# First quad of the feed-forward pass prepared in the last steps of the image pass, its global net beside layer 1 (vision tower, one core)

## The reference, cut to what matters

```
h = h + attention(layernorm(h))        # 16 heads of 16, low-rank projections, causal softmax
x = layernorm(h)                       # feed-forward pass starts here
gf = sigmoid(gelu(gelu(mean_t(x) @ gc_w1 + gc_b1) @ gc_w2 + gc_b2) @ gc_w3 + gc_b3)   # global net
out = x
for _ in range(3):                     # cycles
    tf = sigmoid(mlp4(out))            # 256 -> 256 -> 128 -> 64 -> 1, gelu between
    coupling = 0.1 + adaptive_range * (0.7 * gf + 0.3 * tf - 0.5) * 2
    out = out + coupling * twist(out)  # twist permutes and negates quarters of the row
h = h + out
```

## Time and profile before

| what | value |
|---|---|
| median of 3 runs | 3767.67 us |
| the profiled execution's own time | 3769.01 us |
| its span | 3767.3 us |
| granted TensorE clock, mean | 0.99 of full speed |
| PE busy | 3644.8 us, 97% |
| DVE busy | 3028.1 us, 80% |
| ACT busy | 2402.5 us, 64% |
| POOL busy | 1830.5 us, 49% |
| share of PE in the chain that ended last | 81% |

### The profile page before, as it was taken

One profiled execution on the slowest core, in us unless ns is written; L12 is line 12 of the kernel. 1 busy time (PEld: TensorE's weight loads), 2 busy tenths in 40 slices (PEclk: granted clock), 3 DMA queues, 4 the chain that ended last, 5 costly groups with the idle time before them and its releaser, 6 DMA issues.

```text
span 3767.3 us, 83941 instructions
## 1 busy us (share of the span) xinstructions
PE 3644.8 (97%) x29710; PEld 2685.5 (71%) x29710; DVE 3028.1 (80%) x7295; ACT 2402.5 (64%) x5698; POOL 1830.5 (49%) x2960
## 2 busy tenths in 40 slices
PE   6999999999999999999999999996999999999998
PEld 5888888888888887888888888874555555555554
DVE  6777777777777777777777777774898998998996
ACT  3777777777777777777777777773455555454454
POOL 3766676666667666666766667664100100100000
PEclk9999999999999999999999999997999999999999
DMA  3444454444444444444444444443221222222211
GB/s 103 132 120 125 125 132 119 124 127 126 122 121 132 120 122 128 127 122 121 132 127 122 124 128 131 120 105 95 64 74 58 80 69 63 79 66 68 79 44 52
DMA packets 200000, 398.18 MB, mean 106 GB/s; under 512 B 28192, under 2 KB 133920, under 8 KB 199584
## 3 DMA queue, kind: packets, MB, share of 16 engines
q1 hardware_dynamic: 199584, 392.81, 38.4%
HBM read 131.80 MB, written 53.26 MB: 49 GB/s over the span
## 4 chain that ended last, share of the span: by engine, by line
PE 81%; DVE 9%; issue 3%; POOL 3%; ACT 2%; DMA 2%; SPq 0%; DVEq 0%; POOLq 0%; ACTq 0%
PE ps L1048 14%; PE ps L1326 11%; PE ps L1135 8%; PE ps L1083 7%; PE ps L1335 6%; PE ps L1096 6%; PE ps L1162 4%; PE ps L1120 4%; PE ps L1169 4%; PE ps L1143 3%; PE ps L1164 3%; PE ps L1350 2%; PE ps L1342 2%; POOL p L473 2%; PE ps L1058 1%
## 5 line engine op out<-in xcount | busy, mean ns | idle before, releaser
L1048 PE MATMUL ps<-xb,w_tok 128*128 128x196 f32 x3072 | 694.8, 350 | 0.8 <-DVE h L773 0.5
L857 DVE TENSOR_REDUCE mx<-ps 128x4 f32<-128x512 f32 x512 | 352.5, 688 | 364.6 <-PE ps L1164 364.6
L1326 PE MATMUL ps<-X,cn_w 128*128 128x394 f32 x1536 | 584.9, 510 | 0.4 <-issue 0.4
L861 DVE TENSOR_REDUCE mx<-ps 69x2 f32<-69x396 f32 x1024 | 528.8, 556 | 0.0
L557 ACT ACTIVATE p<-ps 128x394 f32<-128x394 f32 x1024 | 454.6, 499 | 76.4 <-PE ps L1096 66.8
L1048 PEld LDWEIGHTS ps<-xb,w_tok 128*128 128x128 f32 x3072 | 487.1, 190 | 1.2 <-DVE h L773 0.8
L537 POOL TENSOR_SCALAR ve<-mv 128x4 f32<-128x4 f32 x64 | 19.8, 310 | 920.4 <-DVE mv L917 920.4
L1326 PEld LDWEIGHTS ps<-X,cn_w 128*128 128x128 f32 x1536 | 274.1, 190 | 250.7 <-issue 95.4
L508 POOL TENSOR_TENSOR h<-h,att 128x256 f32<-128x256 f32 (+1 forms) x256 | 186.8, 749 | 533.5 <-DVE att L850 533.5
L1169 PE MATMUL ps<-kZ,qT 128*69 128x396 f32 x1024 | 397.2, 454 | 0.1
L1096 PE MATMUL ps<-qZ,kT 128*128 128x396 f32 (+1 forms) x2048 | 380.4, 319 | 11.3 <-DMA qZ<-mx_scratch 8.4
(11 more groups left out here) (140 smaller groups left out, 8238.4 us busy)
## 6 DMA issues: line engine op xcount, KB each, us to landing
kZ<-kT SPq DMA_DIRECT2D x512, 198.0 KB, 3.6
qZ<-qT SPq DMA_DIRECT2D x256, 396.0 KB, 4.7
xb<-in_x SPq DMA_DIRECT2D x128, 588.0 KB, 6.6
h_scratch<-h SPq DMA_DIRECT2D x128, 128.0 KB
hl<-h_scratch SPq DMA_DIRECT2D x64, 256.0 KB
hk<-h_scratch SPq DMA_DIRECT2D x64, 256.0 KB
out<-hk SPq DMA_DIRECT2D x64, 256.0 KB
h_scratch<-h SPq DMA_DIRECT2D x128, 69.0 KB
```

Of the source, the lines that this page charges most:

```text
L857: v.tensor_reduce(mx[:, 0, 4 * i:4 * i + 4], ps[:, b0, :].rearrange("p (a b) -> p a b", b=P), AX.X, ALU.max, negate=True).then_inc(s_max, 1)
L861: v.tensor_reduce(mx[:T1, 1, 4 * i + 2 * jj:4 * i + 2 * jj + 2], ps[:T1, b, 0:2 * TE].rearrange("p (a b) -> p a b", b=TE), AX.X, ALU.max, ...
L1048: mm = t_.matmul(ps[:, W[ft], 0:NP], w_tok[:, k, ft * P:ft * P + P], xb[:, par, k, :], start=k == 0, stop=k == KT - 1)
L1326: mm = t_.matmul(ps[:, 2 * c + mt, 0:N2], cn_w1[:, f, mt * P:mt * P + P], X[:, c, state(cyc), f, :], start=f == 0, stop=f == FT - 1)
```

## The change

SP issues the `hl` loads of quad 0 at the end of step B-2, when the h1 stores of images 0 to 7 are known to have landed; they go to SBUF space of their own, as do `hn2`, `st2`, `ve2`, `rstd2`. DVE does `stats2(0, 0..3)` and `apply2(0, 0..1)` in step B+1 behind `attend`, and `apply2(0, 2..3)` in step B+2 behind the last `attend`. POOL does `norm2(0, 0..1)` in step B+1 in front of the four `select` and `norm2(0, 2..3)` behind them. PE waits for the last `att_ready` before its first `x_transpose`, since the PSUM banks are shared. The three layers of the first global net move into the first phase, between layer-1 and layer-2 matmuls, on PSUM banks given by `GB0`; the wait for g_ready moves to the second phase. The `hk` loads stay behind the wait for all h1 stores.

```diff
--- before.py
+++ after.py
@@ -154,13 +154,7 @@
-        hl = sb("hl", [P, 4, 2, 2, D])
-        st2 = sb("st2", [P, 4, 4, 6])
-        ve2 = sb("ve2", [P, 4, 4])
-        rstd2 = sb("rstd2", [P, 4, 4])
-        hn2 = sb("hn2", [P, 4, 4, D])
-
@@ -174,6 +168,12 @@
+
+        hl = sb("hl", [P, 4, 2, 2, D])
+        hn2 = sb("hn2", [P, 4, 4, D])
+        st2 = sb("st2", [P, 4, 4, 6])
+        ve2 = sb("ve2", [P, 4, 4])
+        rstd2 = sb("rstd2", [P, 4, 4])
@@ -266,6 +266,8 @@
 
         QUADS = B // 8
 
+        GB0 = ((5, 6), (7, 4), (5, 6))
+
         def phases():
 
             for i in range(QUADS):
@@ -360,6 +362,11 @@
...
+            def load2(dst, i, c, s):
+                for t in range(2):
+                    src = h1_dram[:, t * P:t * P + TS[t], :].rearrange("(g n) p d -> g p n d", n=2)
+                    sp.dma_start(dst[0:TS[t], c, t, :, :], src[i * 4 + c]).then_inc(s[c], 16)
+
@@ -378,19 +385,17 @@
                 if there(n + 5):
                     sp.wait_ge(tok_done, n * 2 + 8)
                     load_x(n + 5, 1 - r % 2)
+                if n == B - 2:
+                    for p2 in range(2):
+                        sp.wait_ge(h1_stored[p2], 16 * 8 + 1)
+                    for c in range(4):
+                        load2(hl, 0, c, hl_loaded)
 
             images(sp, step)
             for par in range(2):
                 sp.wait_ge(h1_stored[par], 16 * B + 1)
 
 
-            def load2(dst, i, c, s):
-                for t in range(2):
-                    src = h1_dram[:, t * P:t * P + TS[t], :].rearrange("(g n) p d -> g p n d", n=2)
-                    sp.dma_start(dst[0:TS[t], c, t, :, :], src[i * 4 + c]).then_inc(s[c], 16)
-
-            for c in range(4):
-                load2(hl, 0, c, hl_loaded)
             for c in range(4):
                 load2(hk, 0, c, hk_loaded)
 
@@ -508,15 +513,28 @@
                     g.tensor_tensor(h1[:M, r % 2, t, :], h[:M, m % 6, t, :], att[:M, t, :], ALU.add)\
                      .then_inc(h1_ready, 1)
 
+            def norm2(i, c):
+
+                wait(mv2_ready[c // 2], i * 8 + 4 * (c % 2) + 4)
+                g.tensor_scalar(ve2[:, c, :], mv2[:, c, :, 1], LN_EPS, None, ALU.add).then_inc(ve2_done[c // 2], 1)
+                pool.wait_ge(ve2_done[c // 2], i * 2 + c % 2 + 1)
+                g.tensor_tensor(rstd2[:, c, :], ve2[:, c, :], power[:, 0:4], ALU.pow).then_inc(rstd2_done[c // 2], 1)
+
             def step(n, r):
                 if there(n - 3):
                     residual(n - 3, (r + 1) % 4)
+                if n == B + 1:
+                    norm2(0, 0)
+                    norm2(0, 1)
                 if there(n):
                     k_weighted(n, r, 0)
                     k_weighted(n, r, 1)
                 if there(n - 2):
                     for i in range(4):
                         select(n - 2, i)
+                if n == B + 1:
+                    norm2(0, 2)
+                    norm2(0, 3)
                 if there(n):
                     k_low_part(n, r, 0)
                     q_low_part(n, r, 0)
@@ -531,14 +549,7 @@
...
-            def norm2(i, c):
...
-            for i in range(QUADS):
+            for i in range(1, QUADS):
                for c in range(4):
                     norm2(i, c)
@@ -656,16 +667,17 @@
                     copy(X[:, c, 0, f, :], ps[:, 2 * c + f, 0:N2]).then_inc(x_ready[c], 1)
 
             def gnet(i, G, l):
-                b = 4 * G
+                b1 = GB0[l][G] if i == 0 else 4 * G + 1
+                b2 = GB0[l][G] if i == 0 else 4 * G + 2
                 act.wait_ge(g_done[G], i * 3 + l + 1)
                 if l == 0:
-                    s.activation(ga1[:, G, :], ps[:G1, b + 1, 0:4], ACT.Gelu, bias=gc_b1[:, 0:1],
+                    s.activation(ga1[:, G, :], ps[:G1, b1, 0:4], ACT.Gelu, bias=gc_b1[:, 0:1],
                                  scale=1.0 / T).then_inc(g_ready[G], 1)
                 elif l == 1:
-                    s.activation(ga2[:, G, :], ps[:G2, b + 2, 0:4], ACT.Gelu, bias=gc_b2[:, 0:1])\
+                    s.activation(ga2[:, G, :], ps[:G2, b2, 0:4], ACT.Gelu, bias=gc_b2[:, 0:1])\
                      .then_inc(g_ready[G], 1)
                 else:
-                    s.activation(gth[:, G, :], ps[:, b + 2, 0:4], ACT.Tanh, bias=gc_b3[:, 1:2], scale=0.5)\
+                    s.activation(gth[:, G, :], ps[:, b2, 0:4], ACT.Tanh, bias=gc_b3[:, 1:2], scale=0.5)\
                      .then_inc(g_ready[G], 1)
 
             def gelu1(i, cyc, c):
@@ -690,28 +702,33 @@
 
             for c in range(4):
                 x_copy(0, c)
-            for l in range(3):
-                for G in range(2):
-                    gnet(0, G, l)
+            def gnet0(start, l):
+                if start:
+                    for G in range(2):
+                        gnet(0, G, l)
 
             for i, cyc, G, oi, ocyc in phases():
                 O = 1 - G
+                start = oi < 0
                 fresh = ocyc == CYCLES - 1 and oi + 1 < QUADS
                 if oi >= 0:
                     gelu3(oi, ocyc, O)
                     if fresh:
                         gnet(oi + 1, O, 1)
                 gelu1(i, cyc, 2 * G)
+                gnet0(start, 0)
                 if oi >= 0:
                     for c in (2 * O, 2 * O + 1):
                         tanh(oi, ocyc, c)
                     if fresh:
                         gnet(oi + 1, O, 2)
                 gelu1(i, cyc, 2 * G + 1)
+                gnet0(start, 1)
                 if oi >= 0 and ocyc == 1 and oi + 1 < QUADS:
                     for c in (2 * O, 2 * O + 1):
                         x_copy(oi + 1, c)
                 gelu2(i, cyc, 2 * G)
+                gnet0(start, 2)
                 if cyc == CYCLES - 1 and i + 1 < QUADS:
                     gnet(i + 1, G, 0)
                 gelu2(i, cyc, 2 * G + 1)
@@ -862,6 +879,26 @@
...
+            def stats2(i, c):
...
+            def apply2(i, c, first):
...
@@ -871,6 +908,14 @@
                     rms_sum(n, 1)
                 if there(n - 3):
                     attend(n - 3)
+                if n == B + 1:
+                    for c in range(4):
+                        stats2(0, c)
+                    apply2(0, 0, True)
+                    apply2(0, 1, True)
+                if n == B + 2:
+                    apply2(0, 2, True)
+                    apply2(0, 3, True)
                 if there(n):
                     rms_small(n)
                 if there(n + 2):
@@ -906,26 +951,6 @@
...
-            def stats2(i, c):
...
-            def apply2(i, c, first):
...
@@ -981,10 +1006,6 @@
                     v.tensor_tensor(y, y, ps[:M, 2 * c + t, :].rearrange("p (n d) -> p n d", n=2), ALU.add)\
                      .then_inc(y_ready[c], 1)
 
-            for c in range(4):
-                stats2(0, c)
-            for c in range(4):
-                apply2(0, c, True)
             for c in range(4):
                 gsums(0, c)
             for G in range(2):
@@ -1301,16 +1322,17 @@
                     mm.then_inc(x_done[c], 1)
 
             def gnet(i, G, l):
-                b = 4 * G
+                b1 = GB0[l][G] if i == 0 else 4 * G + 1
+                b2 = GB0[l][G] if i == 0 else 4 * G + 2
                 if l == 0:
                     pe.wait_ge(gsum_ready[G], i * 2 + 2)
                     for f in range(FT):
-                        mm = t_.matmul(ps[:G1, b + 1, 0:4], gc_w1[:, f, :], gsum[:, G, f, :], start=f == 0,
+                        mm = t_.matmul(ps[:G1, b1, 0:4], gc_w1[:, f, :], gsum[:, G, f, :], start=f == 0,
                                        stop=f == FT - 1)
                 else:
                     pe.wait_ge(g_ready[G], i * 3 + l)
-                    mm = t_.matmul(ps[:G2, b + 2, 0:4], gc_w2[:], ga1[:, G, :], start=True, stop=True) if l == 1 else \
-                        t_.matmul(ps[:, b + 2, 0:4], gc_w3r[:], ga2[:, G, :], start=True, stop=True)
+                    mm = t_.matmul(ps[:G2, b2, 0:4], gc_w2[:], ga1[:, G, :], start=True, stop=True) if l == 1 else \
+                        t_.matmul(ps[:, b2, 0:4], gc_w3r[:], ga2[:, G, :], start=True, stop=True)
                 mm.then_inc(g_done[G], 1)
 
             def layer1(i, cyc, c, f):
@@ -1362,18 +1384,23 @@
                                               X[:, c, state(CYCLES), f, n * T + t * P:n * T + t * P + M], ident[:, :])
                     mm.then_inc(y_done[c], 1)
 
+            pe.wait_ge(att_ready, 2 * B)
             for c in range(4):
                 x_transpose(0, c)
-            for c in range(4):
-                pe.wait_ge(x_ready[c], 2)
-            for l in range(3):
-                for G in range(2):
-                    gnet(0, G, l)
-            for G in range(2):
-                pe.wait_ge(g_ready[G], 3)
+
+            def gnet0(start, l):
+                if start:
+                    for c in (2, 3):
+                        pe.wait_ge(x_ready[c], 2)
+                    for G in range(2):
```

(8 more changed lines are left out.)

36 lines of the change are left out of this document (16 added, 20 removed).

## The result

The changed kernel takes 3755.53 us (median of 5 runs, 3755.38 to 3758.79), the kernel before in the same comparison 3770.06 us (5 runs, 3766.25 to 3778.0). The ratio is 0.9966, 95% interval 0.9955 to 0.9978: faster, by 0.34%. The forecast was 3756.6 us, range 3750 to 3762, which is 11.1 us less than before; the medians are 14.5 us apart.

The account below looks back on a forecast made before the run. PE, busy 97%, was taken as the bound, with one large hole at the seam. 18.2 - 1.8 - 4.0 - 1.0 - 0.3 = 11.1 us off 3769.0 gave 3757.9, by the median 3756.6 us; range 3750 to 3762.

Parts of the forecast that it names:

- Term 1: Seam between image pass and feed-forward: layer 1 of cycle 1 earlier, limited by quad 1's hl loads; 18.2 us gained.
- Rival B: At the seam: quad 1's loads flow faster and don't hold DVE; 15.8 us gained, 3751.9 us; chance 0.05.
- Term 2: Layer 1 of cycle 1: PE at low clock behind the new gap in front of it; 1.8 us lost.
- Rival D: Feed-forward pass: the new gap leaves PE at half clock for whole phases; slower, 3777.2 us; chance 0.04.
- Term 3: Step B-2: the mx_scratch store waits behind eight hl loads on SP's queue, delaying scoresT; 4.0 us lost.
- Rival A: Step B-2: small transfers pass the loads, so the store doesn't wait; 16.1 us gained, 3751.6 us; chance 0.11.
- Term 4: Scores and pv behind scoresT: low clock after the longer gap in front of scoresT; 1.0 us lost.
- Term 5: Step B+1: POOL's two norm2 in front of select make PE's selects late; 0.3 us lost.

Follow-up runs that it names:

- the repeat of after: The changed kernel run again without edits, beside three further kernels on the same chip: 3751.88 us against 3766.59 for the kernel before, ratio 0.9963.
- the repeat of before: The kernel before the change, run once more without edits for its profile: 3767.96 us (one run).
- the norms late: The changed kernel with quad 0's statistics, norm2 and apply2 back behind the last attend, loads still early: 3757.34 us against 3769.06, ratio 0.997.
- the global net alone: The changed kernel with quad 0's loads, statistics and norms back behind the image pass, global net still beside layer 1: 3767.84 us, ratio 0.9988.
- the loads alone: The changed kernel with loads, statistics and apply2 early, but the first global net back before the first layer 1: 3758.95 us against 3771.14, ratio 0.9964.

## Why the prediction was right

**Term 1, right in size and reason.** Forecast 18.2 us, measured 18.09, in the repeat of after 18.8. The limit was named right: the hl pairs of quad 1 hold DVE, and x0_new sets PE's start. Taking away 1.93 us by which the last attend was later, layer 1 of cycle 1 ran at 2644.2 against the 2644.1 forecast. Moving those pairs ahead took the gap away, as it must. Counted from the last attend PE was there 1.6 us earlier than forecast, so its gap is 8.77 us and not some 7. Rival B is out: the pairs keep their pace (2.77 us from one to the next).

**Term 2, right reason, too small by 0.9 us.** 1107.67 - 1105.01 = 2.66 us lost against 1.8. The kernels whose clock stayed high behind their gaps of 0.40 and 2.93 us lose nothing (1105.03 to 1105.15), so it is the clock behind this gap. The term was mis-sized because it took 7.74 us for 16 matmuls less 5.96 from a record that began at 2642.05, when the clock had been low since 2639.7. Behind the new gap PE ran from its first matmul on at 0.50, for 5.4 us from 2646.13 to 2651.5, where layer 1 takes twice as long (2.99 us for 1.49); half of 5.4 is the 2.7 lost. Rival D (whole phases at half clock) is out: the pass from cycle 1 on is 2.7 us longer, not over 4. Its price was too low, since it took 0.58 us for a layer-1 instruction at half clock against 0.37, and the rows show twice the time.

**Term 3, too small by 0.7 us, and its mechanism wrong in one step.** scoresT starts 8.93 us behind the store's issue (2557.97 to 2566.90) against 4.23 before: 4.7 us lost, forecast 4.0, upper bound 4.5. The end of the traffic was mis-sized, at 2562.0 instead of some 2563.3. The step that failed is "in the same queue behind the loads": right about the wait, it is too narrow about the reason, for in the one trace with the loads in another queue the store waited until their traffic ended too. Rival A (small transfers pass) is out for SP's queue, by five traces with the store at 5.95 to 6.54 us.

**Term 4, 1.0 forecast, 0 measured.** From scoresT's start to the next mx_scratch issue 14.47 us before, 14.32 after. Two parts cancel. The longer gap let the kZ pads land first, so the wait for kZ vanished, and scores start 4.01 us behind scoresT instead of 4.98. The low clock over the first scores (until 2573.0) then cost 0.8 us, 10.31 to the next store issue against 9.49. In the repeat of after the clock had risen before scores, and the whole is 13.53: 0.9 us gained. I had kept the wait for kZ, though the longer gap covers it.

**Term 5, 0.3 forecast, 0.39 measured**: from the last mx_scratch issue to the end of attend it took 14.44 or 14.45 us in all eight traces with early norms, in which the clock had risen by then. With late norms it took 14.05 and 14.06 in the two traces with the clock up (the repeat of before, and the kernel with the norms late), and 15.74 and 15.51 in the two with it still at 0.50 (before, and the global net alone). The third pair of value matmuls, at 2609.41, stands 0.3 us behind its turn, which is the select. Whether early norms also keep the clock up, eight times of eight against two of four, these runs can't tell.

**What the profile held that was no part of the change.** The terms make 18.1 - 2.7 - 4.55 (step B-1 as a whole) - 0.4 = 10.5 us, where 11.1 were forecast (those of the repeat of after make 18.8 - 2.6 - 3.7 - 0.4 = 12.1). The two profiles differ by 13.5. The rest: step B was 2.2 us shorter and the last stretch, without term 5, 1.7 us; the steps before were 0.9 us longer. The repeat of before shows the first two in a kernel without the change (17.47 and 14.05), and its trace says why: the first profile of before had the clock at 0.50 over scores in step B and over the value matmuls at the end, 1.9 and 1.7 us. The medians are 14.5 us apart in the first comparison, 14.7 in the repeat, 12.2 with the loads alone, 11.7 with the norms late. How often their executions have such low stretches isn't known, so the part of the 14.5 us that the 10.5 don't cover stays open. So does the length of the mx_scratch store in step B: 3.11 to 3.65 us in six of the kernels, with the loads early and late, and 1.4 in the others.

**What was luck.** The forecast of 3756.6 us lies 1.1 us from the measured 3755.53, because two errors cancel: it was taken from a median of 3767.67 us, and before in the comparison had 3770.06, while the gain was 14.5 us and not 11.1. The terms themselves, 10.5 against 11.1, are close in the sum because terms 2 and 3 were too small by 1.6 us and term 4 too large by 1.1.

## What to carry to other kernels

Work moved ahead of a seam is worth what the next transfer in the queue allows: before moving arithmetic, put the loads in the order in which they are waited for (here 7.8 us by the medians, for two lines that change places). A small store that the next step waits for landed here behind the bulk traffic issued before it (6.13 us against 1.38), and in the one trace with the bulk on another queue it didn't get through sooner than that traffic ended either; what helped was to spread the bulk so that it is short (64 + 5 rows for 69: 1.48 us). A gap of 8.77 us in front of PE cost about 2.6 us more than its length in the clock; a shorter gap can be free (2.93 us) or not (2.42 us cost 1.8), so read the clock behind it. And before a difference between two profiles is put down to the change, compare the clock in each stretch: here it made 1.9 and 1.7 us between two executions of one program.

## What the runs showed of the hardware

- The shape of one DMA sets the rate: a pair with a 69-row DMA takes 2.8 to 2.9 us at a DMA share of 0.20, the same bytes with 64 + 5 rows 2.04 us.
- Issuing isn't free, and its price varies: eight issues 5.84 us at the seam and 8.90 in step B-2; two of ACT's took 4.89 us.
- A gap of 2.93 us left the clock high, one of 2.42 was followed by 3.3 us at half clock, one of 8.77 by 5.4 us, in which fp32 layer 1 took 2.99 us for 1.49.
- DVE and POOL are slower side by side, in apply2 and in select and norm2 (pow 1.70 for 1.06 us; eight tensor_scalar 3.93 for 2.6). The tiles' new addresses aren't the cause: with the same addresses and late norms 16 took 5.23 us, as before. By the Trainium skill ("SBUF — State Buffer", section "SBUF: two separate sides") the two engines share a pair of SBUF ports, which one of them holds for a whole instruction, VectorE only in some of its instructions. The trace agrees that both get slower; that it is these ports no run shows.
- The same stretch of the same program took 14.05 us in one execution and 15.74 in another, by a clock that rose at 2603.7 in the one and stayed at 0.50 until 2608.9 in the other, so a term of 2 us wants more than one profile.
